# Sum transfers moved behind the row of maxima, narrow value products, and seven score banks at the end of self-attention

## The reference, cut to what matters

```python
x = x + self_attention(layernorm(x))     # softmax over 512 keys, 16 heads of 8
x = x + cross_attention(layernorm(x), ctx)   # softmax over 32 keys, 16 heads of 8
x = x + ffn_stack(layernorm(x))          # 6 layers: windowed attention, 16 heads of 64, then gated MLP
# self_attention, per batch b and head h
scores = q @ k.T / sqrt(8); attn = softmax(scores); out = attn @ v; out = out.reshape(B, S, D) @ Wo.T
```

## Time and profile before

| What | Value |
|---|---|
| median of 3 runs | 2017.09 us |
| the profiled execution: its own time, its span | 2019.15 us, 2017.3 us |
| busy over the span: PE, DVE, ACT, POOL | 95%, 80%, 65%, 50% |
| 83.00 to 220.50 us: PE, DVE, ACT busy | 127.41, 122.75, 113.67 of 137.50 us, clock 0.95 |
| 251.90 to 347.27 us: PE, DVE, ACT busy | 81.06, 54.51, 38.64 of 95.37 us, clock 0.96 |

### The profile page before, as it was taken

The page is one execution under the profiler, slowest core; times in us unless marked ns, Lnnn a source line. Parts: engine busy times, 40 slices in busy tenths (PEclk is TensorE's granted clock), DMA queues, the critical chain, the costliest instruction groups (busy, mean ns, idle before and its releaser), DMA issues.

```text
span 2017.3 us, 46975 instructions
## 1 busy us (share of the span) xinstructions
PE 1912.3 (95%) x19006; PEld 1152.2 (57%) x19006; DVE 1621.9 (80%) x1822; ACT 1304.4 (65%) x1864; POOL 1016.6 (50%) x743
## 2 busy tenths in 40 slices
PE   6799788899999999999999999999999999999987
PEld 3222145566666666666666666666666666666656
DVE  5898256788888888898889888888888898879773
ACT  3398734567666766676667667766776676667754
POOL 6201133665555555555555556555655565556440
PEclk9899999899999999999999999999999999999999
DMA  3340010354433453335443335443445343343431
GB/s 112 68 78 11 13 40 27 88 135 114 106 94 102 126 136 89 98 100 130 123 105 104 102 97 140 110 109 91 114 121 130 93 104 94 103 124 94 110 104 36
DMA packets 106070, 195.55 MB, mean 97 GB/s; under 512 B 14432, under 2 KB 34912, under 8 KB 105600
## 3 DMA queue, kind: packets, MB, share of 16 engines
q1 hardware_dynamic: 105856, 192.55, 37.0%
HBM read 124.49 MB, written 54.79 MB: 89 GB/s over the span
## 4 chain that ended last, share of the span: by engine, by line
PE 69%; DVE 6%; issue 5%; POOL 2%; ACT 1%; POOLq 0%; ACTq 0%; DVEq 0%
PE ps L1518 13%; PE ps L1598 8%; PE ps L1527 8%; PE ps L1587 8%; PE ps L1542 6%; PE ps L1619 6%; PE ps L1564 6%; PE ps L1575 4%; PE ps L1552 4%; PE ps L1631 3%; DVE l_norms L1934 1%; PE ps L1606 1%; DVE l_o_tok L2002 1%; DVE l_mx L1982 1%; DVE l_rot_s L1955 1%
## 5 line engine op out<-in xcount | busy, mean ns | idle before, releaser
L1491 POOL TENSOR_TENSOR l_rot<-l_rot,l_rot_s 128x1024 f32<-128x1024 f32 x192 | 455.6, 2373 | 27.5 <-DVE l_rot_s L1955 27.5
L1480 POOL COPY l_kb<-l_kb 128x512 f32<-128x512 f32 x95 | 61.5, 647 | 641.9 <-ACT l_kb L1773 641.9
L1494 POOL TENSOR_TENSOR l_rot<-l_rot,l_norms 128x1024 f32<-128x1024 f32 x192 | 365.6, 1904 | 15.1
L1747 ACT ACTIVATE l_sq<-ps 128x1024 f32<-128x1024 f32 x192 | 196.2, 1023 | 183.0 <-PE ps L1518 178.6
L1943 DVE TENSOR_TENSOR l_rot<-ps,l_tab_c 128x1024 f32<-128x1024 f32 x192 | 233.7, 1217 | 36.8 <-ACT l_sq L1747 36.8
L1955 DVE TENSOR_TENSOR l_rot_s<-ps,l_tab_s 128x512 f32<-128x512 f32 x384 | 245.6, 681 | 0.0
L1934 DVE TENSOR_REDUCE l_norms<-l_sq 128x16 f32<-128x1024 f32 x192 | 232.2, 1209 | 0.0
L1542 PEld LDWEIGHTS ps<-l_kb,l_qT 128*32 128x32 f32 x6144 | 163.1, 110 | 76.0 <-issue 44.1
L1773 ACT ACTIVATE l_kb<-ps 64x1024 f32<-64x1024 f32 x192 | 195.5, 1018 | 1.7 <-PE ps L1527 0.6
L1542 PE MATMUL ps<-l_kb,l_qT 128*32 128x128 f32 x6144 | 189.0, 275 | 3.8 <-issue 2.9
L1564 PE MATMUL ps<-l_vb,l_pT 128*32 128x128 f32 x6144 | 188.2, 273 | 3.9 <-issue 2.2
(11 more groups left out here) (191 smaller groups left out, 3238.3 us busy)
## 6 DMA issues: line engine op xcount, KB each, us to landing
l_vb<-v_scratch SPq DMA_DIRECT2D x336, 256.0 KB, 4.8
v_scratch<-l_v_tok SPq DMA_DIRECT2D x96, 512.0 KB, 6.0
l_vb<-v_scratch SPq DMA_DIRECT2D x48, 192.0 KB, 3.2
xsT<-xT SPq DMA_DIRECT2D x48, 135.8 KB, 2.5
l_xf<-xT SPq DMA_DIRECT2D x46, 128.0 KB, 2.3
stack<-scratch SPq DMA_DIRECT2D x72, 64.0 KB
l_wqkv_odd<-wqkv SPq DMA_DIRECT2D x9, 512.0 KB, 6.6
scratch<-parts SPq DMA_DIRECT2D x12, 256.0 KB, 5.6
```

The costliest lines, as they stand in the source:

```text
L1491: nc.gpsimd.tensor_tensor(rot[:, t % 2, n], rot[:, t % 2, n], rot_s[:, n], ALU.add).then_inc(added, 1)
L1494: nc.gpsimd.tensor_tensor(rot[:, t % 2, n], rot[:, t % 2, n], norms[:, t % 2, n, :, None].broadcast_to([P, HEADS, DH]), ALU.mult).then_inc ...
L1747: nc.scalar.activation(sq[:, 1 - r], slot(name, t).rearrange("p n (h d) -> p (n h) d", d=DH), ACT.Square).then_inc(squared, 1)
```

## The change

The gathering of the sums is a function of its own and stays where it was; the inverse's store and spread come one half later, behind that half's rows. POOL's memset of `inv` comes after the first `split_max`. From score 216 on (the last 40) the scores use banks 4, 5, 6, 0, 1, 2, 3 in turn. Cross-attention's value products write 32 partitions each.

```diff
+    WIDE_FROM = 4 * ((HALVES * NM - AHEAD) // 4 + 2)
+    WIDE = (4, 5, 6, 0, 1, 2, 3)
+    def score_bank(n):
+        return 4 + n % SLOTS if n < WIDE_FROM else WIDE[(n - WIDE_FROM) % len(WIDE)]
...
-    def spread_inverse(sp, b):
+    def gather_sums(sp, b):
         sp.wait_ge(o_read, GROUPS * (b + 1))
...
+    def spread_inverse(sp, b):
         sp.wait_ge(inv_out, b + 1)
         sp.dma_start(sums_scratch[b], small[:, b, :]).then_inc(inv_in, 16)
...
-        pool.memset(inv[:, :, :], 1.0).then_inc(inv_set, 1)
         for half in range(HALVES):
             split_max(half)
+            if half == 0:
+                pool.memset(inv[:, :, :], 1.0).then_inc(inv_set, 1)
...
+            if half >= 4 and half % 2 == 0:
+                spread_inverse(sp, half // 2 - 2)
             if half >= 3 and half % 2:
-                spread_inverse(sp, half // 2 - 1)
+                gather_sums(sp, half // 2 - 1)
+        spread_inverse(sp, BATCH - 2)
...
-            if n >= SLOTS:
-                pe.wait_ge(e_ready, n - SLOTS + 1)
+            if n == WIDE_FROM:
+                pe.wait_ge(m_read, len(order))
+            behind = SLOTS if n < WIDE_FROM + SLOTS else len(WIDE)
+            if n >= behind:
+                pe.wait_ge(e_ready, n - behind + 1)
...
-                        m = nc.tensor.matmul(ps[:, 7, i * P:(i + 1) * P], vb[:, b, g, :], pT[:, g, i * P:(i + 1) * P],
-                                             start=(g == 0), stop=(g == GROUPS - 1))
+                        own = slice(32 * g, 32 * g + 32)
+                        m = nc.tensor.matmul(ps[own, 7, i * P:(i + 1) * P], vb[:, b, g, own], pT[:, g, i * P:(i + 1) * P],
+                                             start=True, stop=True, skip_group_check=True)
```

More of the change, by code:

```diff
@@ L635, in scores @@
                 pe.wait_ge(laid, 64 * (n // NM + 1))
-            if n >= SLOTS:
-                pe.wait_ge(e_ready, n - SLOTS + 1)
+            if n == WIDE_FROM:
[3 more added lines that the diff above has]
+                pe.wait_ge(e_ready, n - behind + 1)
             h = 4 * g + j
             c = h // 2
-            nc.tensor.matmul(ps[:, 4 + n % SLOTS, :], stack[rows(h), b, 1, c, kt * P:(kt + 1) * P],
+            nc.tensor.matmul(ps[:, score_bank(n), :], stack[rows(h), b, 1, c, kt * P:(kt + 1) * P],
                              stack[rows(h), b, 0, c, :], start=True, stop=True).then_inc(s_ready, 1)
@@ L716, in scalar @@
                 act.wait_ge(pv_group, (n - RING) // 4 + 1)
-            nc.scalar.activation(probs[:, n % RING, :], ps[:, 4 + n % SLOTS, :], ACT.Exp,
+            nc.scalar.activation(probs[:, n % RING, :], ps[:, score_bank(n), :], ACT.Exp,
                                  scale=float(DK) ** -0.5).then_inc(e_ready, 1)
```

## The result

The changed kernel takes 1999.41 us (median of 4 runs, 1993.32 to 2002.82), the one before 2017.32 (4 runs): a ratio of 0.9909 with a 95% interval of 0.9882 to 0.9936, so 18 us or 0.9% faster. The forecast was 1997.6, with 1991.5 to 2004. The profiled execution of the changed kernel was its fastest run, 1993.32 us with a span of 1991.5, so its span must not be compared with the one before as a whole.

| Stretch | before | after | forecast |
|---|---|---|---|
| start to the first turn | 73.6 | 68.3 | -1.7 |
| first turn to the first score | 9.4 | 9.5 | +0.7 |
| first score to group 52 | 137.6 | 126.9 | -11.1 |
| group 52 to the cross-attention | 31.6 | 28.3 | -2.3 |
| cross-attention | 95.1 | 91.0 | -5.1 |

The account below looks back on a forecast made before the run. PE was taken as the bound over most of the span, DVE in groups 0 to 51, ACT in 52 to 63. Terms -11.1 - 1.0 - 2.3 - 5.1 = -19.5 us took 2017.09 to 1997.6 us; range 1991.5 to 2004.

Parts of the forecast that it names:

- The two late rows: Self-attention, halves 4 and 6: rows no longer queue behind the sums' store and spread; 5.5 and 5.6 us, -11.1 us.
- What the moved spread meets: POOL's product ahead of the splits of halves 5 and 7: later spread costs nothing, covered by 2.2 and 1.9 us.
- The memset: POOL ahead of the first split: without the memset the first turn starts earlier; -1.0 us, bounds -0.3 and -1.3.
- Seven banks: Groups 52 to 63: four scores issued together, ACT becomes gapless; 7 gaps of 0.33 us, -2.3 us.
- Narrow value products: Cross-attention: eight records take 0.35 us on PE, not 0.89; -5.1 us, 2.5 in the loop and 2.6 after it.
- Rival A: Cross-attention: narrow products bring nothing or PE's gaps grow until the clock falls, about 1.7 us each; 2002 to 2003; chance 0.14.
- The sum: Whole kernel: the terms give -19.5 us, all before the layers, so 1997.6 us for the median.

Follow-up runs that it names:

- the late spread: The changed kernel with the store of the inverses done four more times before each spread, making it some 5.9 us later: 2004.62 us, ratio 0.9937.
- the run of the wide products: The changed kernel without the narrow value products, with four full-width products of 128 columns that add up instead: 2001.98 us, ratio 0.9927.
- the change once more: The changed kernel run and profiled again with no edit: 1998.52 us, ratio 0.9908.
- the gap filled: The changed kernel with two unread fp32 products of 512 columns at each of two PE gaps in the cross-attention: 1997.67 us, ratio 0.9895.
- the run with both additions: The changed kernel with filling products at two cross-attention gaps and half 2's rows ahead of the store of batch 3's parts: 1993.94 us, ratio 0.9883.

## Why the prediction was right, point by point

- **The two late rows (-11.1).** Right: 10.7 in the first pair of profiles, 10.0 when undone. The split of each 5.5 us was off, though not its sum: 0.84 of the 4.41 us stand ahead of the score of every half, late rows or not, so the late rows added 3.6 us of wait, and 1.9 and not 1.1 lie behind it. What was left out is a third row that can be late, that of half 2. In the trace before, its step was 3.49 us and cost nothing (0.84 us, with the transfer named as releaser); in other executions it made the largest difference in this stretch.
- **What the moved spread meets (nothing).** Right, with 2.35 and 2.19 us of cover for the 2.2 and 1.9 worked out; the late spread showed what lies beyond it.
- **The memset (-1.0).** Right in size as far as profiles tell, and in its reason for the range: 1.74 us at the turn, 0.9 on average at the first score. The profile named DVE as the releaser of a wait that ended with POOL's split; undoing it showed which.
- **Seven banks (-2.3).** Right mechanism, size 3.3. The mis-sized term is what a gap costs. Exponents overlap: sixteen in a row start 0.48 us apart (216.54 to 224.17), though one by itself takes 0.60. So the row of four in 2.06 us is about 3 x 0.48 + 0.60, and a group without a gap takes 4 x 0.48 = 1.91 us, not 2.06. A gap that is shown as 0.33 us costs 2.39 - 1.91, and the seven of them 3.3. PE's group was put at 1.98 us, with 0.22 for each score. It is 1.61, 1.00 for the products and 0.61 for four scores, and then PE waits 0.40. At 1.98 PE would have been the bound, and part of the gain would not have come.
- **Narrow value products (-5.1).** Right mechanism, size 4.0 to 4.4. The table's 4.1 is the difference of two blocks with like falls of the clock; others can be compared only after sorting them by these.

  *Up to the output product.* From the block's start to the output product of batch 2 the clock is at half for 3.4 us, for 6.8, or for 6.8 and later 3.4 more. These take 81.1, 82.7 and 82.8 to 82.9 us with wide products and 78.6, 79.8 to 80.1 and 80.3 with narrow ones: 2.5 to 2.9 less, 2.5 forecast. (One more with narrow products, at half for 3.4 and later for 3.4 more, took 79.4 and has no partner.)

  *From there to the layers.* Here the forecast had 2.6 less, and this term is mis-sized. With wide products, first with the fall of the clock behind the gap of 2.2 us (the kernel before) and then without it (the run of the wide products):

```profile
333.32:347.30 13.98, 13.67 (x60) 9.41 (x61) 2.62 (x5) 4.63 (x9) 4.52 (x3) 0.88 0.00 0
320.96:333.30 12.34, 12.02 (x60) 7.77 (x61) 2.61 (x5) 4.65 (x9) 4.54 (x3) 1.00 0.00 0
```

  With narrow ones, again with the fall (the change) and without it (the change once more):

```profile
311.68:324.14 12.46, 12.13 (x61) 5.43 (x61) 2.62 (x6) 4.63 (x9) 4.54 (x3) 0.87 0.00 0
320.97:331.90 10.93, 10.61 (x60) 4.77 (x61) 2.61 (x5) 4.54 (x9) 4.54 (x3) 1.00 0.00 0
```

  Like for like that is 1.5 and 1.4 us for four sets, some 0.36 each, where the forecast had 0.5 for three of them and 1.1 for one at half clock. The 0.35 us of a set (0.36 measured) left out what the instructions around it pay, 0.1 us on either side, as the rows of the run with wide products show. And the set at half clock brought nothing more: the half clock lasted 3.4 us with either kind of product, so the narrow ones only let other work fall into it. The prediction had named a price of this kind: twice the 0.14 for going in and out, it said, would take 1.4 us from the 5.1. By the rows it is 0.15 inside the set and 0.19 around it. That the loop still gained what the forecast had, with a smaller saving for each set, is not worked out.
- **Rival A, the clock.** It did not come: a fall behind the gap costs 1.5 to 1.7 us with wide products and with narrow ones, near the 1.7 of the rival, but narrow products do not bring it. It came in two of the four profiles with wide products and in five of the seven with narrow ones and no filling, behind a gap as long in all (2.19 to 2.21 us). The four profiles without it had a fall of 3.4 us some 24 us behind the block's start instead, and the seven others had none there. With the gap filled both profiles kept the full clock, but one of them had that early fall (at 22 us). So only the run with both additions speaks for the filling. The block's 91.3 us in the repeated change is this too: 1.7 us more than in the first profile up to the output product, 1.5 less behind it.
- **The sum.** 19.7 us by the stretches that the change touches, 18 us by the medians, 19.5 forecast. That the sum came so close is in part luck: the banks brought 1.0 us more than their term and the narrow products about as much less. The 5.3 us of the table's first line hold 1.7 of the change. The layers' 2.6 us are not explained: in the profiles of all kernels the ranges with and without the change touch, and it stays open whether some 1.5 us of it are real.

## What to carry to other kernels

An issue queue that runs in order is to be read like an engine: what is wanted first must not stand behind a transfer that waits for another engine, and five small DMAs in the wrong place cost 10 us here. When something is moved behind it, work out what waits for the moved part, and find its room in the idle time of the engine that takes it; that number held within 0.3 us. For changes of a few us cut the profiles at common instructions and compare stretches, as the times of one kernel differ by more than the terms. Before a stretch is compared, look where the clock fell in it: a fall that costs 1.5 us came here in some executions of either kernel and not in others, and only like pairs show what a change brought.

## What the runs showed of the hardware

- Exponents of 128x512 from PSUM that follow each other without a gap start 0.48 us apart, though one takes 0.60 (sixteen in 7.63 us). So an idle time shown as 0.33 us between them costs 0.46 to 0.48 us, and the time of a short row must not be taken for its share of a long one.
- Eight narrow fp32 records of 128 columns, placed alone between full-width products, take 0.36 us of their own and make the products on either side some 0.1 us longer. So a set costs about 0.55 us, against 0.89 for eight full-width ones and 0.21 for eight inside a run of 64.
- Behind a gap of one length (2.19 to 2.21 us) the clock fell to half for 3.4 us in seven of the eleven profiles without filling, at the first product behind it in five and a product later in two, and not at all in four. Where it fell, the 11 to 14 us behind the gap took 1.5 to 1.7 us longer. The gap's length alone does not tell.
- The changed kernel's start, up to the first turn, took 68.3 and 72.7 us in its two profiles, a larger difference than in any stretch behind it (3.1 us at most).
